# Row maxima spread by VectorE's time per block, and row sums of the last head group's second half taken on TensorE: causal attention in a conditioned transformer layer

## What is computed

```python
mod = silu(condition) @ Wada + bada            # shifts, scales, gates
xm  = layernorm(x) * (1 + sc_a) + sh_a
q, k, v = split_heads(xm @ Wqkv)               # 16 heads, 32 wide
scores  = where(causal, q @ k.T * hd**-0.5, -inf)
x = x + gt_a * (merge_heads(softmax(scores) @ v) @ Wproj + bproj)
xm = layernorm(x) * (1 + sc_m) + sh_m
x = x + gt_m * (gelu(xm @ W1 + b1) @ W2 + b2)
```

## Time and profile before

| | us |
|---|---|
| median of 3 runs | 2444.97 (2442.23 to 2445.43) |
| the profiled execution | 2443.25 |
| its span, first to last instruction | 2441.5 |
| TensorE matmul busy | 2278.1 (93%) |
| VectorE busy | 1285.3 (53%) |
| ScalarE busy | 906.3 (37%) |
| GpSimd busy | 866.9 (36%) |

### The profile page before, as it was taken

The page is one execution under the profiler, slowest core; times in us unless marked ns, Lnnn a source line. Parts: engine busy times, 40 slices in busy tenths (PEclk is TensorE's granted clock), DMA queues, the critical chain, the costliest instruction groups (busy, mean ns, idle before and its releaser), DMA issues. The chain is left out here.

```text
span 2441.5 us, 37678 instructions
## 1 busy us (share of the span) xinstructions
PE 2278.1 (93%) x11655; PEld 1510.8 (62%) x11655; DVE 1285.3 (53%) x2886; ACT 906.3 (37%) x1740; POOL 866.9 (36%) x355
## 2 busy tenths in 40 slices
PE   6999968999999899999999999798799999999998
PEld 5888844444445445444444445476588888888887
DVE  6656457676777668676776740467431221222122
ACT  2111103555555556555655554210432222222221
POOL 0000024756677575667767575363000000000000
PEclk9999966998999999899999986799899999999999
DMA  5454465126162432615243121375420110110110
GB/s 181 166 194 171 149 181 122 44 54 140 46 131 49 95 69 54 140 46 119 51 108 77 44 45 53 123 248 190 159 91 9 52 52 0 52 52 0 52 34 17
DMA packets 129055, 223.28 MB, mean 91 GB/s; under 512 B 8448, under 2 KB 25912, under 8 KB 128828
## 3 DMA queue, kind: packets, MB, share of 16 engines
q1 hardware_dynamic: 105660, 175.18, 26.9%
q10 hardware_dynamic: 23232, 46.14, 5.2%
HBM read 145.26 MB, written 76.02 MB: 91 GB/s over the span
## 5 line engine op out<-in xcount | busy, mean ns | idle before, releaser
L815 ACT ACTIVATE prob<-st 128x512 f32<-128x512 f32 (+3 forms) x1280 | 611.9, 540 | 466.7 <-PE st L985 445.0
L789 POOL TENSOR_TENSOR psum_k<-psum_k,prob 128x2048 f32<-128x2048 f32 (+1 forms) x128 | 576.3, 4502 | 55.4 <-ACT prob L815 48.7
L966 PE MATMUL mx<-k_st,qx_st 96*128 96x512 f32 (+1 forms) x1249 | 511.4, 430 | 48.7 <-DMA k_st<-qk_scratch 21.4
L863 DVE TENSOR_REDUCE part<-mx 128x1 f32<-128x512 f32 x744 | 457.4, 681 | 131.5 <-PE mx L966 129.0
L985 PE MATMUL st<-q_st,k_st 98*128 98x512 f32 (+3 forms) x1280 | 496.5, 403 | 13.9 <-issue 8.3
L966 PEld LDWEIGHTS mx<-k_st,qx_st 96*128 96x128 f32 x1249 | 248.5, 200 | 216.0 <-DVE part L863 99.9
L985 PEld LDWEIGHTS st<-q_st,k_st 98*128 98x128 f32 x1280 | 253.1, 199 | 181.3 <-issue 123.3
L1525 DVE TENSOR_TENSOR m_g_lo<-m_g,m_g_hi 128x512 fp32r<-128x512 f32 x128 | 88.6, 693 | 511.9 <-ACT m_g_hi L1489 511.3
L859 DVE CUSTOM_DVE_ANT_0 unused<-mx,mask_row 128x512 bf16<-128x512 f32 (+2 forms) x505 | 226.5, 488 | 152.5 <-PE mx L966 117.6
L1002 PE MATMUL o_ps<-prob,v_sb 128*32 128x512 f32 (+3 forms) x2560 | 304.4, 586 | 0.0
L1485 ACT ACTIVATE m_g<-m_hid,vcol 128x512 f32<-128x512 f32 x128 | 88.3, 690 | 495.8 <-PE m_hid L1617 495.7
(11 more groups left out here) (155 smaller groups left out, 2569.7 us busy)
## 6 DMA issues: line engine op xcount, KB each, us to landing
qx_st<-qk_scratch SPq DMA_DIRECT2D x96, 256.0 KB, 4.7
k_st<-qk_scratch SPq DMA_DIRECT2D x96, 256.0 KB, 8.2
q_st<-qk_scratch SPq DMA_DIRECT2D x96, 256.0 KB
qk_scratch<-st_hi ACTq DMA_DIRECT2D x16, 1024.0 KB, 4.2
qk_scratch<-st_lo ACTq DMA_DIRECT2D x16, 1024.0 KB, 6.4
xs<-in_x_dram SPq DMA_DIRECT2D x8, 1024.0 KB, 5.3
v_scratch<-st_v ACTq DMA_DIRECT2D x8, 1024.0 KB, 4.3
v_sb<-v_scratch SPq DMA_DIRECT2D x8, 1024.0 KB, 15.4
```

Of the source, the lines that this page charges most:

```text
L789: nc.gpsimd.tensor_tensor(dst, src, prob[:, s % BUF, :, m:], ALU.add).then_inc(pool_added, 1)
L815: nc.scalar.activation(prob[:, s % BUF, h, m:], st[n % RING][:, m:], ACT.Exp, scale=SCALE).then_inc(exp_done, 1)
L863: nc.vector.tensor_reduce(most, bank[:, 0:w], AX.X, ALU.max).then_inc(mx_free, 1)
L966: nc.tensor.matmul(out[:, 0:w], qx_st[0:ROWS, pos % 2, h, t * P:(t + 1) * P], k_st[0:ROWS, u, h, kc * CH:kc * CH + w], start=True, stop=Tr ...
```

## The change

It does two things. The prices of the items become estimates of VectorE's time (800 for a turn, 610 for a full item, 190 + 0.85 ns a column for a triangle), and the weight of a block becomes its scores' time plus at most 1700 ns of product phase, less 750 in the block of a sum transpose and 1700 in that of a norm. And in the last group, chunk 2 pools only the tiles 0, 1, 4, 7 and chunk 1 none. The bookkeeping of the sums moves into a class `Sums`, one object for the groups with a successor (the old table) and one for the last.

```diff
+class Sums:
+    def __init__(self, plan, pooled):
+        self.plan, self.pooled = plan, pooled
+        self.adds, self.released, done = [], [], 0
...
+    def added(self, pos):
+
+        return self.pooled[self.plan.order[pos]] != ()
...
     POOLED = {3: (0, 1, 2, 4, 5, 6, 8, 9, 10, 12), 2: (0, 1, 2, 4, 5, 6, 8, 9), 1: (0, 1, 2, 4), 0: ()}
+    POOLED_LAST = {3: (0, 1, 2, 4, 5, 6, 8, 9, 10, 12), 2: (0, 1, 4, 7), 1: (), 0: ()}
...
+        self.sums = {True: Sums(self, self.POOLED), False: Sums(self, self.POOLED_LAST)}
+        self.NA = self.sums[True].NA
...
-        price = [300 if isinstance(it, int) else it[4] + 70 for it in work]
+        price = [800 if isinstance(it, int) else 610 if it[3] != self.order[it[0]] else 190 + 0.85 * it[4] for it in work]
...
         ns = sum(GH * max(self.width(s) / 2.4 + 13, 200) for s in own)
-        ns += sum(1.67 * self.width(s) * (2 if self.direct(s) else 1) + 170 for s in (2 * b - 2, 2 * b - 1))
-        return ns + 870 * (b - 1 in self.last_block[:-1]) - 500 * (self.normed(b) is not None)
+        ns += min(1700, 340 + sum(1.67 * self.width(s) * (2 if self.sums[True].direct(s) else 1) for s in (2 * b - 2, 2 * b - 1)))
+        return ns - 750 * (b - 1 in self.last_block) - 1700 * (self.normed(b) is not None)
...
-                if L.direct(s):
-                    opens = L.first_direct(s)
+                if L.sums[more].direct(s):
+                    opens = L.sums[more].first_direct(s)
...
-            def total(g, s, pos):
-                if pos == QC - 1:
+            def total(g, s, pos, more):
+                if not L.sums[more].added(pos):
```

More of the change, by code:

```diff
@@ L406, in _, with direct, first_direct, first_add @@
             wave(nc.tensor, body, NCH)
+class Sums:
+    def __init__(self, plan, pooled):
+        self.plan, self.pooled = plan, pooled
+        self.adds, self.released, done = [], [], 0
+        for s, (pos, kt) in enumerate(plan.steps):
+            chosen = pooled[plan.order[pos]]
+            if kt not in chosen:
+                self.released.append(done)
+            elif kt == chosen[0]:
+                self.released.append(done + 1)
+            else:
+                done += 1
+                self.adds.append(s)
+                self.released.append(done)
+        self.NA = done
+    def direct(self, s):
+        pos, kt = self.plan.steps[s]
+        return kt not in self.pooled[self.plan.order[pos]]
+    def first_direct(self, s):
+        pos, _ = self.plan.steps[s]
+        return self.direct(s) and not any(self.direct(r) for r in range(s) if self.plan.steps[r][0] == pos)
+    def first_add(self, s):
+        pos, kt = self.plan.steps[s]
+        return kt == self.pooled[self.plan.order[pos]][1]
+    def added(self, pos):
+        return self.pooled[self.plan.order[pos]] != ()
 class Plan:
     POOLED = {3: (0, 1, 2, 4, 5, 6, 8, 9, 10, 12), 2: (0, 1, 2, 4, 5, 6, 8, 9), 1: (0, 1, 2, 4), 0: ()}
+    POOLED_LAST = {3: (0, 1, 2, 4, 5, 6, 8, 9, 10, 12), 2: (0, 1, 4, 7), 1: (), 0: ()}
     def __init__(self):
@@ L486, in norm @@
         return not isinstance(it, int) and it[0] == "norm"
[L488 to L494, removed]
     def diagonal(self, s):
@@ L773, in select, with add @@
                                         pattern=[[0, GH], [1, P]], channel_multiplier=-1).then_inc(masked, 1)
-            def add(g, s):
-                n = L.adds.index(s)
+            def add(g, s, more):
+                n = L.sums[more].adds.index(s)
                 pos, kt = L.steps[s]
@@ L782, in add @@
                     pool.wait_ge(masked, mask_count(g, L.selects.index(s) + 1))
-                if kt == L.POOLED[L.order[pos]][1]:
+                if L.sums[more].first_add(s):
                     pool.wait_ge(r_ready, r_count(g, 1 if pos == 2 else -1))
@@ L794, in body @@
                         select(g, s)
-                    if s - 1 in L.adds:
-                        add(g, s - 1)
+                    if s - 1 in L.sums[more].adds:
+                        add(g, s - 1, more)
             per_group(nc.gpsimd, body)
@@ L804, in _, with exps @@
             act.sem_inc(o_copied, 1)
-            def exps(g, s):
+            def exps(g, s, more):
                 m = L.mid(s)
                 act.wait_ge(pv_done, pv_count(g, s + 1 - BUF))
-                n = L.released[s - BUF] if s >= BUF else L.released[s - BUF] - L.NA
+                n = L.sums[more].released[s - BUF] if s >= BUF else L.sums[True].released[s - BUF] - L.NA
                 act.wait_ge(pool_added, add_count(g, n))
@@ L829, in body @@
                         if s < L.NS:
-                            exps(g, s)
+                            exps(g, s, more)
                         elif more:
-                            exps(g + 1, s - L.NS)
+                            exps(g + 1, s - L.NS, more)
                         if not more and s in LOAD_AT:
@@ L841, in _ @@
             load_ada(1)
-            exps(0, 0)
-            exps(0, 1)
+            exps(0, 0, True)
+            exps(0, 1, True)
             per_group(nc.scalar, body)
@@ L987, in scores, with product @@
                     between(h)
-            def product(g, u, s):
+            def product(g, u, s, more):
                 pos, kt = L.steps[s]
@@ L1009, in product @@
                         ins = nc.tensor.matmul(r_ps[h * HD:(h + 1) * HD, m:], K.ones[:, 0:HD], prob[:, s % BUF, h, m:],
-                                               start=opens, stop=end and pos == QC - 1)
+                                               start=opens, stop=end and not L.sums[more].added(pos))
                 ins.then_inc(pv_done, 1)
                 if end:
-                    total(g, s, pos)
-            def total(g, s, pos):
-                if pos == QC - 1:
+                    total(g, s, pos, more)
+            def total(g, s, pos, more):
+                if not L.sums[more].added(pos):
                     pe.wait_ge(pv_done, pv_count(g, s + 1))
@@ L1019, in total @@
                     return
-                n = sum(r <= s for r in L.adds)
+                n = sum(r <= s for r in L.sums[more].adds)
                 pe.wait_ge(pool_added, add_count(g, n))
@@ L1056, in body @@
                     for s in (2 * b - 2, 2 * b - 1):
-                        product(g, u, s)
+                        product(g, u, s, more)
                     if not more:
```

## The result

| | median of the runs | against the kernel before, 95% interval |
|---|---|---|
| before | 2444.57 us (20 runs) | |
| changed | 2449.88 us (20 runs) | 1.0020 (1.0012 to 1.0029) |

The change costs 5.3 us, about the least that can be told from nothing here. The sign was forecast and the time lies in the range, but 15.3 us were forecast, three times as much.

What follows compares the result with a forecast made beforehand. TensorE's own order of work was taken as the bound. Terms 7.7 + 1.6 + 7 - 1 = 15.3 on the profiled 2443.25 gave 2458.6; with the runs' median 1.7 higher, the forecast was 2460 us, range 2442 to 2480.

Steps and rivals of the forecast that it cites:

- S: Length of a block's score phase, the part before its product phase; a floor of about 3.5 us, rising with items.
- The ramp of 0.59 us an item: Score phase from about 7 full items on: VectorE paces TensorE, and one more item costs VectorE 0.59 us.
- forecast +1.1: Items' new places, net per group in the first seven: losses of +5.3 us against gains of -4.2.
- I count -1 in all for: Clock falls in blocks 7 and 8: the stretch ahead gets shorter and a little thinner, worth -1 us in all.
- the 7 us of the direct sums: Last group, blocks 10 to 18: added matmuls on TensorE's path cost 5.8 us at full clock, up to 9.0, taken as 7.
- the third rival: Clock falls in new places, blocks 3 and 4 or the norm blocks; one more a group gives +19, 2479 us; chance 0.15.
- +7.7 - 1: First seven groups: the items' new places cost 7.7 us, the clock gives back 1.
- +1.6: Eighth group, blocks 1 to 8, the only ones there with items: the new places cost 1.6 us.
- VectorE's pace wasn't milder: Rival: 0.34 us an item, not 0.59, and added sums hiding under ScalarE, -7 us each, giving 2446; chance 0.12.
- S(9): Score phase of a block with 9 full items: forecast about 4.93 us, with ends at 4.67 and 5.2.
- GpSimd didn't hold the eighth group up: Rival: GpSimd held the eighth group up, so dropping seven adds shortens it, giving 2441 us; chance 0.03.
- The first rival: Clock no longer falls in blocks 7 and 8, gaining 5.4 us per group where both had fallen; chance 0.10.

Runs made afterwards that it cites:

- steady_old: Kernel before, with useless matmuls filled into TensorE's waits in blocks 7 and 17 and ahead of turns T3 and T0: 2412.46 us, 0.9862 of before.
- steady_new: Kernel before with only the items' new places, plus the same useless matmuls as in steady_old: 2428.38 us, 0.9925 of before.
- places_only: Kernel before with only the items' new prices and block weights, the last group's row sums pooled as before: 1.0019 of before.
- sums_only: Kernel before with only the last group's direct sums, old item prices and block weights: 1.0014 of before.
- both_again: The whole changed kernel once more, on the same chip as its two parts: 1.0029 of the kernel before.
- ramp_mods: Changed kernel's item order with a table of items per block, old row sums, and the last group's modulation matmuls between the scores: 2383.18 us, 0.9749 of before.
- fill_b7: Kernel before with six useless zero-weight matmuls between the scores of block 7 in every group: 0.9943 of before.

## Why the prediction was off

**What held.** S in the mean over groups two to seven, in us:

| block | 5 | 11 | 12 | 13 | 2 | 20 | 9 | 14 | 4 | 18 | 19 |
|---|---|---|---|---|---|---|---|---|---|---|---|
| before | 3.98 | 3.98 | 3.92 | 3.09 | 4.51 | 3.57 | 4.58 | 4.34 | 4.42 | 4.58 | 3.77 |
| after | 4.94 | 4.94 | 4.94 | 4.22 | 4.95 | 3.98 | 3.58 | 3.98 | 5.34 | 3.99 | 2.27 |
| forecast change | +0.9 | +0.9 | +0.9 | +1.2 | +0.4 | +0.4 | -1.1 | -0.35 | +0.5 | -0.35 | -0.9 |
| measured change | +0.96 | +0.96 | +1.02 | +1.13 | +0.44 | +0.41 | -1.00 | -0.36 | +0.92 | -0.59 | -1.50 |

The ramp of 0.59 us an item holds wherever it was used. The three wrong terms (4, 18, 19) cancel to within 0.4. Block 10 went from 8 to 10 items, and the prediction has no term for it; S rose by only 0.09 there. The 20 blocks' length, in the mean over the same groups, went from 138.1 in `steady_old` to 139.5 in `steady_new`: +1.4 a group, +1.2 where the clock was full in both, forecast +1.1. Other signs came as well: in the first seven groups the items' weight loads waited 97.8 us for full items' maxima (84.4 before) and ScalarE 396.2 us for scores (381.6 before). GpSimd wasn't nearly idle in the eighth group's blocks 9 to 20, though: it was busy for 20 of 94 us.

**The steps that failed: "I count -1 in all for" the clock, and the 7 us of the direct sums, of which the prediction says "I take 7, since 0.67 is two thirds of the way to half".** Both take TensorE's clock as all but what it was before. Part one measured +4 against a forecast of 8.3, part two +4 by the runs and 2.9 in its stage against 7. Each run lists its mean granted clock over the span. In 50 runs of the kernel before it moved between 0.936 and 0.943, and the time with it: 0.001 of clock is 1.6 us (19 runs at 0.938 took 2446.2 on average, 15 at 0.940 took 2442.6, 6 at 0.942 took 2439.7). With that slope, taken over to the other kernels as an estimate (within the runs of each other kernel the slope lies between 1.2 and 2.3, so the clock's part may be off by a third):

| | clock, mean of runs | time against before (means) | the clock's part | the rest | forecast without the clock |
|---|---|---|---|---|---|
| places_only | 0.9430 (before 0.9396) | +4.0 | -5.5 | +9.6 | +9.3 |
| sums_only | 0.9425 | +3.8 | -4.8 | +8.6 | +7 |
| both_again | 0.9469 | +6.8 | -11.9 | +18.7 | +16.3 |

So the work that the change puts on TensorE's path was sized nearly right, and the clock gave back some 12 us, not 1. The steady pair shows the same for part one without the slope: at full clock it costs 8.4 us in seven groups and 1.9 in the eighth, 10.3 for the forecast's 9.3, where `places_only` measured 4.

Where it gave back: for part two, in blocks 9 to 14 of the eighth group. I priced its matmuls at the clock that stood there before (0.67, "two thirds of the way to half"), as if it were fixed. It isn't: with them it stands at 0.78 in `sums_only` and at 0.80 in the change. A mean clock of 0.67 between 1.00 and half says that TensorE stood at half clock for 2 x (1 - 0.67) x 61.80 = 41 us; in `sums_only` it is 2 x (1 - 0.78) x 61.87 = 27. So blocks 9 to 20 cost 2.9 us more and not 7. For part one, blocks 7 and 8 together went from 19.9 to 17.7 us in the mean over groups two to seven, product phases included; block 8's products ran at full clock in every group. The items taken out are worth 1.0 of these 2.2 (the steady pair; forecast 1.3). The other 1.2 a group are the clock's, some 8 us in seven groups, where the forecast's -1 stood for all seven together. Against that, blocks 16 and 17 went from 16.4 to 18.0: the third rival, falls in new places, came true in part, in 16 or 17 of each of the first seven groups where before it was three of them (and not in blocks 3 and 4, where the rival looked for them). In the single profiled executions these two nearly cancel; that part one's clock is higher in the mean of the runs is measured, and which block makes it so isn't settled.

The windows of `both_again`, whose profiled execution (span 2447.8) is typical:

```profile
397.20:1392.80 995.60, 948.98 (x5686) 473.20 (x5685) 695.88 (x1761) 558.99 (x1150) 671.29 (x246) 0.95 0.36 80
1392.80:1451.20 58.40, 55.66 (x317) 26.45 (x317) 39.27 (x111) 33.46 (x66) 43.94 (x14) 0.97 0.21 47
1451.20:1511.50 60.30, 58.51 (x349) 31.02 (x345) 4.27 (x8) 22.68 (x49) 14.59 (x7) 0.80 0.18 54
1511.50:1545.20 33.70, 31.83 (x234) 13.51 (x233) 2.90 (x6) 16.29 (x42) 5.10 (x8) 0.90 0.04 16
```

By stage, against before's: start of attention -2.0, seven groups +5.4 (forecast +7.7 - 1; 8.4 at full clock), the eighth's blocks 1 to 8 +1.3 (+1.6), blocks 9 to 14 -1.5, 15 to 20 +2.8 up to the last direct sum (the last two +7 together): +6.0. So of the 9 us that are missing from the forecast, 4 are the price of the direct sums, 1.6 the falls of blocks 9 to 14 that came less under the new places alone, 1.3 the seven groups, 0.3 the eighth's blocks 1 to 8, and 2.0 the start, for which the forecast has no term.

The first group's block 1 began at 397.2 to 397.7 us in the four kernels with the new places, and at 398.5 to 400.2 in the seven that keep the old ones. The new places issue three early items fewer ahead of it. That is the likely reason, but no run changes it alone, and `ramp_mods`, with one fewer, began at 397.9 as well, so I leave it open.

**The rule on the penalty.** By the Trainium skill, page "TensorE: Matmul & The Clock Gate", section Terms, throttled time costs half of itself at half rate, so 0.001 of mean clock would be 2.4 us. The 50 runs say 1.6, as would be if a third of the half-clock time went on waits for others, which no run here tests. In blocks 7 and 8 the prediction's rows had 5.4 for the rule's 6.8, the same direction.

**The other rivals.** VectorE's pace wasn't milder (S(9) is 4.94, not 4.67). GpSimd didn't hold the eighth group up: without its seven additions blocks 9 to 20 got longer. The first rival came true by half: in both profiled executions of the change block 7 fell in each of the first seven groups and block 8 in none (in `places_only` it fell in one).

## What to carry to other kernels

Where a stage runs partly at half clock, don't price matmuls put into it at that stage's clock: here they came with a higher one, and the stage took no longer. Before moving or adding work there, put useless matmuls into TensorE's short waits once, to see what the clock is worth (33 us of 2445 here), and then look for real work to put there: the small modulation matmuls between the scores shortened their stage by 14 of 62 us. Compare variants of such a kernel by the time and the mean clock of many runs, since a profiled execution lay up to 4.8 us from the median of its kernel's runs (`steady_old`).

## What was unexpected of the hardware

- Blocks 9 to 14 of the eighth group show TensorE busy for 60.71 of 61.80 us at a clock of 0.67, and for 58.54 of 60.35 at 0.80 after. The busy column doesn't tell a reader that the clock is low; the clock column has to be read beside it.
- Six matmuls with zero weights in block 7 held the clock at 1.00 through this block in all eight groups of `fill_b7` (8.16 us for 10.51 in the third), and through the next one in three of them (8.12 for 10.82 in the third).
- A fall that is taken away tends to come back at another thin place: block 16 or 17 fell in three of seven groups before, and in five once 7 was filled.
- Two kernels with the same code in the first seven groups differ by up to 3 us there (990.2 before, 993.4 in `sums_only`); the blocks that differ are those in which falls come.
